# Other merge tables for the four threads of each engine, in a two-layer encoder kernel on one core

## The reference

```python
x = x + 0.5 * _L0_ffn_ref(_layernorm(x), ...)   # norm, 128->512, gelu, norm, 512->128
x = x + _L0_attn_ref(_layernorm(x), ...)        # 16-state scan over time, gated by gelu(z)
x = x + 0.5 * _L0_ffn_ref(_layernorm(x), ...)
x = x + 0.5 * _L1_ffn_ref(_layernorm(x), ...)   # sigmoid encoder, router, top 2 of 8 experts, decoder, norm
x = x + _L1_attn_ref(_layernorm(x), ...)        # conv of 3 taps, selective scan of 256 channels x 16 states in chunks of 32
x = x + 0.5 * _L1_ffn_ref(_layernorm(x), ...)
```

## Time and profile before

| | |
|---|---|
| median of three timed runs | 1179.11 us (1177.35 to 1183.39) |
| the profiled execution | 1166.19 us, of which the span of instructions 1164.5 us |
| granted TensorE clock, mean | 0.922 |
| busy: PE, DVE, POOL, ACT | 1028.6, 785.3, 669.2, 650.5 us |
| DMA | 176.69 MB, mean 152 GB/s |
| ACT table loads at L980 | 76, 97.5 us |

### The profile page before, as it was taken

How to read it: one execution, slowest core, us unless ns; L and a number is a source line. 1 busy time by engine, 2 the same in 40 slices (tenths; PEclk the granted TensorE clock), 3 DMA queues, 4 the chain that set the end, 5 groups by cost and what they waited for, 6 DMA issues and landing times.

```text
span 1164.5 us, 12622 instructions
## 1 busy us (share of the span) xinstructions
PE 1028.6 (88%) x4164; PEld 556.4 (48%) x4164; DVE 785.3 (67%) x1564; ACT 650.5 (56%) x1021; POOL 669.2 (57%) x572
## 2 busy tenths in 40 slices
...
GB/s 117 10 1 82 1 27 131 216 144 187 137 160 164 110 208 110 179 201 182 217 154 160 176 120 170 242 164 204 160 250 161 233 203 242 197 207 242 109 82 10
DMA packets 55721, 176.69 MB, mean 152 GB/s; under 512 B 7332, under 2 KB 17896, under 8 KB 51560
## 3 DMA queue, kind: packets, MB, share of 16 engines
...
...
## 4 chain that ended last, share of the span: by engine, by line
PE 50%; DVE 14%; POOL 13%; ACT 10%; issue 6%; DMA 4%; SPq 1%; POOLq 0%; DVEq 0%; ACTq 0%
PE yp L1464 11%; POOL dbu L654 5%; PE mp L1349 4%; PE mp L1339 4%; PE fp L1253 4%; PE fp L1247 4%; DMA bcast<-held 3%; PE fp L1232 3%; PE pp L1378 3%; DVE dA L949 3%; PE pp L1308 2%; PE pp L1313 2%; PE yp L1446 2%; ACT a_z L997 2%; ACT L980 2%
## 5 line engine op out<-in xcount | busy, mean ns | idle before, releaser
L654 POOL TENSOR_TENSOR dbu<-du,bcast 128x1024 f32<-128x1024 f32 x128 | 302.7, 2368 | 148.3 <-DMA bcast<-held 78.8
L1464 PE MATMUL yp<-hs,ident 128*128 128x512 f32 x512 | 276.3, 673 | 32.3 <-DVE hs L956 25.7
L949 DVE TENSOR_TENSOR_SCAN dA<-dA,dbu 128x512 f32<-128x512 f32 x192 | 226.3, 1215 | 66.1 <-ACT dA L1191 44.7
L1191 ACT ACTIVATE dA<-delta,mA 128x496 f32<-128x496 f32 x256 | 165.9, 669 | 133.0 <-DVE dA L959 101.6
L1464 PEld LDWEIGHTS yp<-hs,ident 128*128 128x128 f32 x512 | 103.2, 214 | 161.5 <-issue 109.3
L882 DVE SCALAR_TENSOR_TENSOR he<-mp,vectors,he 128x512 f32<-128x512 f32 x128 | 89.6, 742 | 50.7 <-PE mp L1339 35.9
L956 DVE TENSOR_TENSOR hs<-dA,bcast 128x1024 f32<-128x1024 f32 x96 | 117.5, 1224 | 4.2 <-PE yp L1464 1.1
L1339 PE MATMUL mp<-cont,w_e 64*128 64x512 f32 x256 | 92.3, 685 | 13.7 <-DVE he L882 12.1
L980 ACT ACT_TABLE_LOAD x76 | 97.5, 1283 | 1.4
L638 POOL TENSOR_TENSOR hs<-hs,bcast 128x1024 f32<-128x1024 f32 x32 | 77.1, 2409 | 33.9 <-DVE hs L949 33.7
L949 DVE TENSOR_TENSOR_SCAN hs<-dA,dbu 128x512 f32<-128x512 f32 x64 | 75.0, 1206 | 18.3 <-ACT dA L1191 17.4
...
## 6 DMA issues: line engine op xcount, KB each, us to landing
bcast<-held SPq DMA_DIRECT2D x128, 1024.0 KB, 5.5
...
```

The lines of the kernel that those rows point to most:

```text
L654: pool.tensor_tensor(out=dbu[:, j % 2, :].rearrange("p (r t) -> p r t", r=2), in0=d, in1=b_n, op=ALU.mult).then_inc(dbu_r.sem, 1)
L949: dve.tensor_tensor_scan(out=h, data0=dA[:, half], data1=dbu[:, j % 2, half], initial=0.0, op0=ALU.mult, op1=ALU.add).then_inc(hs_r.sem, 1)
L1191: act.activation(out=dst, in_=src, func=ACT.Exp, scale=mA[:, c, n:n + 1]).then_inc(dA_r.sem, 1)
L1464: last = pe.matmul(yp[:, :], lhsT=ident[:, :], rhs=hs[:, j % 2, r * SEQ:(r + 1) * SEQ], start=(k == 0 and r == 0), stop=(k == PAIRS - 1 an ...
```

## The change

Only the five strings of `ORDER` differ. They were found by a longer search of the same kind as those before. Each string has as many letters of each thread as before; threads, steps, buffers and waits are the same. Beginning of two of them (SP, and PE's first lines; the other lines change alike):

```diff
     "SP":
-        "AGAGGBBBBABBBGBGGBBBBBBAGGGBBBBBBBBBBBGBGGBABBBGGGBBBBBBBBBDBABBGBGGBBBGBBBBBBBGGBBBBBGBGGBBDGABBBGG"
...
+        "AGAGGBBBBABBGGGBBBBBBGGGABBBBBBBBBBBBGBGGBBABBGBBBBBBGGBBBBBBBBGBGGDBABGBGGBBBBBBBBBBBGBGGBDBBBGBBAB"
...
     "PE":
-        "FFSFFFAFFFFFSSSSSSSSSSSSSSSSSSSSSSSSFSSSFSSSSFSSSSSSSSSSSSSSSSSSSSSSSSSSSSSSSFSSSSSSSSSSSSSSSSSSSSS"
...
+        "FFSFFFAFFFFFSSSSSSSSSSSSSSSSSSSSSSSFSSFSSSFSSSSSSSSSSSSSSSSSSSSSSSSSSSSSSSFSSSSSSSSSSSSSSSSSSSSSSSFS"
...
```

More of the change, by code:

```diff
@@ L39 @@
     "SP":
-        "AGAGGBBBBABBBGBGGBBBBBBAGGGBBBBBBBBBBBGBGGBABBBGGGBBBBBBBBBDBABBGBGGBBBGBBBBBBBGGBBBBBGBGGBBDGABBBGG"
-        "BBBBBBBBDBBGBGGBBBBBGBBBBGGBBBBBBBBBBGBGGBBDBGBBBBBBBGGBBBBBBBBBGBGGBBBBBBBBDBBBBBBGBGGBDBBBBBDGGGD",
+        "AGAGGBBBBABBGGGBBBBBBGGGABBBBBBBBBBBBGBGGBBABBGBBBBBBGGBBBBBBBBGBGGDBABGBGGBBBBBBBBBBBGBGGBDBBBGBBAB"
+        "GGBBBBBBBDBBBBBGBGGBGBGGBBBBBBDBBBBBBGBGGBBBGBBBBBBBGGBBBBBGBGGBBDBBBBBBBBBBBBBBBBDBBBGGGBBBBBDGGGD",
     "Pool":
-        "FFFFFFFFFAFAFFFFFBBAAFFFAFFAFSSASASFSSFSFSFFASASSSBSBFSFFASSASFSFASSASSSFSAFASSFSBBSFSFAFSSASFSFASAB"
@@ L44 @@
-        "SBSFSSFASFSASSAABSBFSFSFSSSASASSFSFASASSSSASSSFASSASFBFSBASSSASBBASAFSSFASFSSAFSSFBSBASFSAFASSFBSBSS"
-        "SSASAFSFSSFSSASASSSSASFSSASFSBSSFBASSASSSASSBBSSAASASSSSASSASSASBSBASSSSSSSSASASSSASSBSSASBSSASASSSS"
-        "SSSBSBSSSSSSSSBBAABB",
+        "FFFFFFFFFAFAFFFFFBBAAFFFAFFAFASSSAFSFSSSSFSAFAFSSBSBAFAFSFSASSSSAFSFBBSSFSASAFSFSSSASAFSSSFSFASASSSS"
+        "ASFSFBSASBSSFASAFSSFSSBBSASFSASFFASSASFSFSASBSBSFASASSFASFSSSBASBAFSSSSAASSSSAFSFBSSBSASSFSFBBSFASSA"
+        "FSFSSSSASFAFFASASAFSFSBASBSBSBSFSASSASSSSSASASSSASASSSSASSSASASSBSBASSASASBBSSSASSSASSSSSSSSSSASSABS"
@@ L47 @@
+        "BSSSSSSSSSSSSSBABABB",
     "DVE":
[L48 to L52, removed]
@@ L53 @@
-        "SSBSSSBSSSBSSSSSAAASSSSSSSSSSSSABSSSBSSSBSSASSSBSSSASASSSBSSSSSSSSSSSSAASSBSSSSSSBSSSBSSBSSSBSSSSSSS"
-        "SSSSBSAAAABBBBB",
-    "ACT":
[L56 to L62, removed]
@@ L63 @@
-    "PE":
[L64 to L72, removed]
+        "FFFFAFAAFFFFFFFFFFAAAFFFBBBBFFFFBAFFFAFFFAASSFSFSFFSSAASSSSSBBBSSBSSFSFAFSSSSSBAASAFFFSSSBSBSSSABSSS"
@@ new lines @@
+        "BFSSFSSSFAFSSBSSSSSSFFASSSSFSSSSSSAASSAASSSSSFSFSSFSSSBASAASSSFSSSBSSSSBSABSSSFSFFSSBSBSSBASSBSBSSSF"
+        "SFASSFSSSSSSSSBAASSSAASSSFSBFSBBFBAASASSSFSSSFSFSFSABSSBSSSBSSSBSSSSSFAFABSSSSFSSSSSSSAABSAASSSSSSFB"
+        "SSBSSAASABSSSSBSSSFSSSASSFSSSBSSSSBBBSBSSSFAFSFSFSBSSSSFSFASSSSFSSSSSSAASSAASSSFBFFBBBAAASSSSFSSSFSF"
+        "ABFBSBBSSBSASSSBSSSSSFSSSFASSSSSSSSSSSSSAASSSAASSBSSSSSBSAASASSBSSSSSSSSSSASBSSSSSSSSASAASSSBSSBSBSS"
+        "SBBAAASSSSSBSSSSSASSSBSSSSBSSSBASSSSSBSSSSSSSSSSSSSSSASSSASSSSSBSSSSSSSSSSSAASSSSSSSBSSBBSSSBSSSSSSS"
```

18 lines of the change are left out of this document (added).

## The result

The changed kernel takes 1189.19 us (median of 20 runs, 1180.8 to 1202.35); the kernel before took 1172.86 beside it (20 runs, 1165.87 to 1190.7). The ratio is 1.0134, 95% interval 1.0105 to 1.0162: slower by 1.3%, where I had forecast faster. Medians are of all runs, but every ratio leaves out a kernel's executions in a slower state that the chip falls into now and then: three of the twenty here (1199.87 to 1202.35 us). The time lies just outside my range's upper end of 1188. My range was drawn on a median before of 1179.11 us; on that scale the measured ratio comes to 1195 us, so the miss is larger than the two times say.

The account below looks back on a forecast made before the run. PE's own work plus its waits was taken to bound 321 to 874 us, then the step loop. Terms summed to -7.5 us, 1166.19 to 1158.7 profiled; scaled by 1.011, 1171 us was predicted, range 1157 to 1188.

Parts of the forecast that it names:

- Before step 0: Ahead of the first scan step: 17 fewer keep-clock matmuls ahead of batch 0's second L1403, -0.5 us, bounds -3.8 and 0.
- Ahead of step 88: On PE before scan step 88: four more transposes for pp and four for the gates, +1.8 us.
- Step 48: PE's 3.52 us wait for a_z shrinks, one dbu ahead of its norm instead of two: -2.3 us.
- step 72: PE's 3.80 us wait for a_z is covered by 5.4 us of ready matmul work: -3.8 us.
- The waits of the work put in: Work inserted at steps 48 and 72 brings its own waits, at PE's 7.5% idle share: +0.7 us.
- everything else reordered: Other reordering between 321 and 874 us: no known sign, zero, a quarter of 34.4 us idle gained or lost (8.6).
- my 33 to 37 us: Sign to check in the profile after: PE idle time between steps 16 and 88.
- Seven table loads: On ACT: 69 function table loads for 76, 26% of each on the path, -2.3 us, bounds -9.0 and 0.
- From step 88: Steps 88 to 127: one routing block less on DVE against foreign work inside steps, -0.7 us, from -5 to +12.
- the rival of step 99: DVE work between step 99's two scans stops scanning 7.9 us: slower, 1189 us; chance 0.18 including the like elsewhere.
- No change: Rival: the waits removed at steps 48 and 72 reappear elsewhere; 1177 us on the median's scale, chance 0.27.
- "slower" case: Outcome above 1185.0 us, by the row of step 99 or the like of it elsewhere; chance 0.18.

Follow-up runs that it names:

- e16: e4 with ScalarE's expert-stage tanh L1102 moved ahead of the three convolution passes, one table load fewer; 1178.03 us, ratio to before 1.0022.
- e4: Order of the kernel before on all five engines up to scan step 88, then the changed order; 1173.15 us, ratio to before 0.997.
- e11: Order of the kernel before on all five engines up to scan step 72, then the changed order; 1186.61 us, ratio to before 1.0095.
- e15: Changed order on all five engines up to scan step 72, then the order of before; 1194.49 us, ratio to before 1.0116.
- e13: Changed kernel with the second part of batch 3's expert stage some 40 us later, into steps 80 to 88; 1199.53 us, ratio to before 1.0197.
- e17: Changed kernel with ScalarE's two exponentials of step 65 moved ahead of the f_z norm; 1194.73 us, ratio to before 1.0113.

## Why the prediction was wrong

*Before step 0: -0.5.* Putting the fillers back (e1) gave nothing that can be told from zero, 1.0139 for 1.0134, which fits a term near zero. The group that I showed did as told: its filler is gone and L1276 starts at 56.82 us for 57.03.

*Ahead of step 88: +1.8 us of PE work.* PE's busy time up to the first scan sum of step 88 is 814.0 us for 809.6, +4.4; the sign was right. How much of the other 2.6 us is the clock's, the trace doesn't tell.

*Step 48, -2.3, and step 72, -3.8.* At step 72 no wait of a_z is left: the transposes come straight behind ready work. At step 48 the wait of 3.52 us didn't shrink, it moved ahead to the expert matmul that the new order puts there: L1344 at 579.46 us waits 2.81 us for L882. My "work that is ready" wasn't.

```profile
579.46 1.07 PE L1344 MATMUL mp<-gT,b_e 8*64 8x512 f32 x2 [2.81 <-DVE he L882]
```

*The waits of the work put in, +0.7, and "everything else reordered", 0 +- 8.6.* This is the step that failed. I charged the new neighbours at PE's mean idle share, 7.5% of 8.7 us, and gave the rest no sign. Measured, PE's idle time between steps 16 and 88 is 54.7 us for 41.7: +13.0, against my 33 to 37 us. The cuts place the loss in steps 56 to 88, where PE idles 11.0 us more up to the same transposes, and 8.3 of that is before transposes of a_z and of the gate. I had followed two waits because the old trace showed them; waits that only the new order has, as the four above, are in no trace of before. That they are the cause, and not one sign of a worse fit among others, no run shows: none takes them out.

*Seven table loads, -2.3.* The 69 loads came true. e16 took a load out of e4 and moved the tanh forward, and gained nothing (1.0022 for e4's 0.997). The runs don't measure the seven alone, so whether the term is zero stays open.

*From step 88: -0.7, and the rival of step 99.* 287.5 us for 290.5, of which the last batch takes 64.5 for 63.5, and e4 is 0.997: the tail is no slower, the rival falls. Its price of 1189 us is the measured time to the microsecond, by luck: it stood for a gap of scans at step 99 and was scaled to a median before that is 6 us above the one measured beside the result. PE's extra work there was hidden as I said: it does 90.96 us in 102 for 76.34 in 96, and its 10.6 us of waits before the scan sums are gone.

*No change* was the nearest of my cases in mechanism (the waits come back elsewhere), and its price was too low: they came back larger. Step 88 is reached at 894 us for 874, where I had it 7 us sooner. My bound for this, a quarter of the idle time, was drawn only around the forecast; in the "slower" case I had a single row and no weight for the plain possibility that a new order fits worse.

What stays open: which half of steps 56 to 88 carries the loss (e11 and e15 disagree by more than their intervals allow for a sum), and whether there is a single cause at all. The place of the loss is shown by the cuts; its mechanism is not. Three repairs that each took one visible wait or misplacement out (e13, e16, e17) didn't make a kernel faster beyond its uncertainty, and e13 made it slower.
